# Attention: the value products of four units in one group on TensorE, with six probability buffers

## The chip, the cores and the metric

The kernel runs on one core of a Trainium2 chip. Its time is the device time of one execution in microseconds, from the first to the last instruction and the little that lies around them. Three engines matter here: TensorE (PE) multiplies matrices and writes to PSUM, VectorE (DVE) takes row maxima, ScalarE (ACT) takes exponentials and copies projections out of PSUM. GpSimd (POOL) prepares blocks of queries, SyncE (SP) issues the DMAs. The engines run their own instruction streams and wait for each other by semaphores.

## The reference, cut to what matters

Four layers, each an attention over 1444 context keys and a feed-forward part, on x of 32 batches x 100 tokens x 128. Three of the four attentions (a0, a1 and a3) have 16 heads of 8 columns and use the code that is changed; a2 is another function. In a0, for each batch:

```python
qh = proj(q, Wq, bq); kh = proj(k, Wk, bk); vh = proj(v, Wv, bv)      # 16 heads x 8
scores = jnp.einsum('bhqd,bhkd->bhqk', qh, kh) / jnp.sqrt(8)
attn = jax.nn.softmax(scores, axis=-1)                                # over 1444 keys
out = jnp.einsum('bhqk,bhkd->bhqd', attn, vh)                         # the value products
return concat @ Wo.T + bo
```

a1 masks keys by an integer mask (zeros take the place of the scores there), and a3 masks by a length per batch.

## The kernel before, in words

`attention_phase` (from L195) is called for a0, a1 and a3, one after the other, with other work between them. Each call goes through 32 batches. A batch has 24 units: two halves of eight heads, and for each half twelve tiles of 128 keys (the twelfth has 36 keys). The loop over units in `block.tensor` (from L926) writes out TensorE's order by hand. In unit u of batch b it issues:

- one maximum product, `max_mm` (L838): queries x 480 or 482 keys, into one of three PSUM banks, the ring `p_mx` (`RING = 3`). VectorE takes the row maximum from the bank (L657 in a0, L665 in a1, L671 in a3) and frees it. These products belong to the unit 16 units ahead (`LEAD`), 48 of them in a batch.
- the scores of the unit, `score_mm` (L853): two products of 400 columns into one of two PSUM slots, `p_sc`. In a1 two small products add the mask (L867). ScalarE then takes the exponential of 128 x 800 into a buffer of `probs` (L550, in a3 L548).
- in some units a small job of the batch before or after: the turned output at unit 2 (L890), `concat_turn` at 5, the output projection at 8 (L902, L904), the negated maxima at 9 and 21 (L835), in a1 `u_proj` at 13 (L827), the projection of queries at 18 (L817). They use the ring `p_mx` too, and VectorE reads them; the longest of these reads is `normalise` (L705), which VectorE does between the two maxima of unit 2.
- the second maximum product.
- in every even unit the value products, `pv_mm` (L871), of the two units before: 4 matmuls a unit, each with 32 columns of weights, side by side in the four column quarters of the array, 200 columns long in f32. In the trace each f32 matmul stands as two, so two units are 16 rows of L879. They add up in one bank, `p_pv`, over a half, and ScalarE copies it out (L536).
- in units 9, 11, 13 and 15 a projection of the next values and keys: `v01` and `v2` (L810), `k0` and `k12` (L803). They go into the two slots `p_sc` too, in turn with the scores, and ScalarE copies them out (L527 for values; L509 or L511 for keys, twice each).

What sets the order of waiting: a product into the ring waits until the third turn before it was read (`ring`, L787). A product into `p_sc` waits until the second turn before it was read (`slot`, L792). The exponential of a unit waits for its scores, and for the value products that last read its buffer:

```python
NP = 4                                                     # L230
wait_some(act, pv_done, at - NP + 1)                       # L543
```

In the text below "unit 12" is the turn of the loop with u = 12, and "a pair" is an even unit with the odd one after it.

Of the kernel before, what the change touches and what calls it, by code (L numbers as in the profile page):

```python
# [14 lines left out]
B = 32  # L15
# [9 lines left out]
UNITS = 2 * KT  # L25
# [26 lines left out]
class Memory:  # L52
# [7 lines left out]
    def sb(self, name, shape, dt=F32):  # L60
        return self.ctx.enter_context(self.nc.sbuf_tensor(f"{self.prefix}_{name}", shape, dt))
# [133 lines left out]
def attention_phase(nc, name, x, xnT, ident, w, dram, scale, gate, mask=None, lens=None):  # L195

    with ExitStack() as ctx:
# [29 lines left out]
        nm = sb("nm", [S, 2, HALF])  # L227
        nmsp = sb("nmsp", [S, 2, 32], F32R)
        nsb = sb("nsb", [D, S])
        NP = 4  # L230
        probs = sb("probs", [D, NP, HALF * S])
        osb = sb("osb", [D, 2, 2 * S])
        rs = sb("rs", [S, 2, HALF])
# [112 lines left out]
        def p_slot(*job):  # L346
            return p_sc[sc_turn[job] % 2]

        def wait_some(eng, signal, count):
            if count > 0:  # L350
                eng.wait_ge(signal, count)

        def full(eng, *job):

            if job in mx_turn:
                eng.wait_ge(mx_full, mx_turn[job] + 1)
            else:
                eng.wait_ge(sc_full, sc_turn[job] + 1)

        def taken(eng, *job):  # L360

            if job in mx_turn:
                eng.wait_ge(mx_free, mx_turn[job] + 1)
            else:
                eng.wait_ge(sc_free, sc_turn[job] + 1)
# [127 lines left out]
        def _(act):  # L493
# [44 lines left out]
            def exps(b, u):  # L538
# [3 lines left out]
                full(act, "exp", at)  # L542
                wait_some(act, pv_done, at - NP + 1)  # L543
                out_ = probs[0:rows, u % NP, :].rearrange("p (g n) -> p g n", g=2)
                in_ = p_slot("exp", at)[0:rows, :, 0:4 * S]
# [237 lines left out]
        def _(pe):  # L783
# [37 lines left out]
            def u_proj(b):  # L821
                to = ring("u", b)
                taken(pe, "v2", b)
                pe.wait_ge(gone_ready, b + 1)
                for t in range(KT):
                    r = D if t < KT - 1 else LAST
                    ins = pe.matmul(to[0:S, 0:HEADS * 9].rearrange("p (h d) -> p h d", h=HEADS),  # L827
                                    gone[0:r, b % 2, t, :], v_aug[0:r, b % 2, t, :, 0:9],
                                    start=(t == 0), stop=(t == KT - 1))
                ins.then_inc(mx_full, 1)  # L830

            def neg_turn(b, h):
                to = ring("neg", 2 * b + h)
                pe.wait_ge(negm_ready, 2 * b + h + 1)
                pe.matmul(to[96:128, 0:S], nmsp[:, h, :].bitcast(F32), ident[0:S, 0:S],  # L835
                          start=True, stop=True).then_inc(mx_full, 1)

            def max_mm(k):  # L838
                b, r = divmod(k, 2 * UNITS)
                if b >= B:  # L840
                    return
                h, r = divmod(r, 2 * KT)
                head, c = divmod(r, NCH)
                o, n = CHUNKS[c]
                if r == 0:
                    pe.wait_ge(stack_in[b % 2][h], (b // 2 + 1) * 96)
                    pe.wait_ge(qblk_ready, 2 * b + h + 1)
                to = ring("max", k)
                g = 2 * h + head // 4
                pe.matmul(to[0:S, 0:n], qblk[0:96, b % 2, HALF * h + head, :], stack[0:96, b % 2, g, o:o + n],  # L850
                          start=True, stop=True).then_inc(mx_full, 1)

            def score_mm(b, u):  # L853
                h, kt = divmod(u, KT)
                r = D if kt < KT - 1 else LAST
                if kt == 0:
                    pe.wait_ge(qneg_ready, 2 * b + h + 1)
                if u == 0 and mask is not None:
                    pe.wait_ge(pen_ready, b + 1)
                to = slot("exp", UNITS * b + u)  # L860
                for g in range(2):
                    out_ = to[0:r, g, 0:4 * S]
                    ins = pe.matmul(out_, stack[:, b % 2, 2 * h + g, kt * D:kt * D + r],  # L863
                                    qblk[:, b % 2, HALF * h + 4 * g:HALF * h + 4 * g + 4, :].rearrange("p h s -> p (h s)"),
                                    start=True, stop=mask is None)
                    if mask is not None:
                        ins = pe.matmul(out_.rearrange("p (h s) -> p h s", h=4), identb[0:r, 0:r],  # L867
                                        bc(pen[0:r, b % 2, kt, :], 1, 4), start=False, stop=True)
                ins.then_inc(sc_full, 1)

            def pv_mm(b, u):  # L871
                h, kt = divmod(u, KT)
                r = D if kt < KT - 1 else LAST
                taken(pe, "exp", UNITS * b + u)
                if kt == 0:
                    wait_some(pe, pv_out, 2 * b + h)
                for t in range(4):
                    head = HALF * h + 2 * t
                    ins = pe.matmul(p_pv[32 * t:32 * t + 32, 0:2 * S],  # L879
                                    v_aug[0:r, b % 2, kt, head:head + 2, :].rearrange("p h d -> p (h d)"),  # L880
                                    probs[0:r, u % NP, 2 * t * S:2 * (t + 1) * S],
                                    start=(kt == 0), stop=(kt == KT - 1))
                ins.then_inc(pv_done, 1)

            def out_turn(b):
                to = ring("out", b)
                pe.wait_ge(pv_out, 2 * b + 2)
                for a in range(2):
                    for h in range(2):
                        ins = pe.transpose(to[0:S, a * 256 + h * D:a * 256 + (h + 1) * D],  # L890
                                           osb[:, h, a * S:(a + 1) * S], ident[:, :])
                ins.then_inc(mx_full, 1)

            def concat_turn(b):
                to = ring("concat", b)
                pe.wait_ge(norm_ready, b + 1)
                pe.transpose(to[:, 0:S], concat[:, :], ident[0:S, 0:S]).then_inc(mx_full, 1)

            def out_proj(b):
                to = ring("wo", b)  # L900
                taken(pe, "concat", b)
                ins = pe.matmul(to[0:S, 0:D], ctsb[:, :], wo[:, :], start=True, stop=bo is None)  # L902
                if bo is not None:
                    ins = pe.matmul(to[0:S, 0:D], ones_row[:, :], bo[:, :], start=False, stop=True)  # L904
                ins.then_inc(mx_full, 1)
# [19 lines left out]
            for b in range(B):  # L925
                for u in range(UNITS):  # L926
                    g = UNITS * b + u + LEAD
                    max_mm(2 * g)
                    score_mm(b, u)
                    if b > 0:  # L930
                        if u == OUT_AT:
                            out_turn(b - 1)
                        if u == CONCAT_AT:
                            concat_turn(b - 1)
                        if u == WO_AT:
                            out_proj(b - 1)
                    if u == NEG1_AT:
                        neg_turn(b, 1)
                    if u == U_AT and mask is not None and b + 1 < B:
                        u_proj(b + 1)  # L940
                    if u == Q_AT and b + 2 < B:
                        q_proj(b + 2)
                    if u == NEG0_AT and b + 1 < B:
                        neg_turn(b + 1, 0)
                    max_mm(2 * g + 1)
                    if u % 2 == 0 and (b > 0 or u > 0):
                        for back in (2, 1):
                            at = UNITS * b + u - back
                            pv_mm(at // UNITS, at % UNITS)
                    if u == V01_AT and b + 1 < B:  # L950
                        v_proj("v01", b + 1)
                    if u == V2_AT and b + 1 < B:
                        v_proj("v2", b + 1)
                    if u == K0_AT and b + 2 < B:
                        k_proj("k0", b + 2)
                    if u == K12_AT and b + 2 < B:
                        k_proj("k12", b + 2)
            pv_mm(B - 1, UNITS - 2)
            pv_mm(B - 1, UNITS - 1)
            out_turn(B - 1)  # L960
            concat_turn(B - 1)
            out_proj(B - 1)
# [1278 lines left out]
```

## Time and profile before

| | |
|---|---|
| median of 3 runs | 6742.71 us (6737.07 to 6746.94) |
| profiled execution | 6736.52 us, span 6734.7 us |
| busy, share of the span | PE 88%, PE weight loads 60%, DVE 70%, ACT 52%, POOL 29% |
| granted TensorE clock, mean | 0.938 |
| a0, a1 and a3 at full clock | about 1283, 1707 and 1348 us |
| value products L879 | 18432 rows, 1051.8 us busy |

A busy share of PE is not PE at its peak: matmuls are pipelined, and the end of one is modelled. What counts in the rows are the starts. In a timeline a row gives its start and length in us, then engine, line, operation, what is written and read, shapes and the number of instructions merged in the row; in brackets how long the engine had been idle before it, and who ended that.

### The profile page before, as it was taken

The page shows a single profiled execution, that of the slowest core. Times are in us where ns is not written, and L with a number is a line of the kernel's source. Part 1 is how long each engine was busy: PE and PEld are TensorE (multiplying, and loading weights), DVE is VectorE, ACT ScalarE, POOL GpSimd, SP SyncE. Part 2 cuts the span into 40 slices and gives each one's busy share as a digit, 9 for nine tenths or more (in the row PEclk, how much of TensorE's full clock was granted, in tenths as well). Part 3 has the DMA queues.
Part 4 walks back from the last instruction along what each step waited for, and adds up shares of the span by engine and source line. Part 5 has one row for each costly group of instructions (what it writes and reads, how often), then busy time and mean ns, then how long its engine had stood idle before and what let it go on. Part 6 is the DMA issues. An engine that isn't in the chain of part 4 may idle for free. (4 is left out here: it accounts for less than half of the span.)

```text
span 6734.7 us, 123692 instructions
## 1 busy us (share of the span) xinstructions
PE 5947.1 (88%) x42776; PEld 4044.1 (60%) x42776; DVE 4732.6 (70%) x12652; ACT 3471.3 (52%) x5250; POOL 1972.7 (29%) x1415
## 2 busy tenths in 40 slices
PE   6999999969897999999999956768498799999996
PEld 4666666659894555555555545645388466566653
DVE  6878777867676666666666676634577777777775
ACT  3666666655553444444444433423255466666664
POOL 2222222224453222222222122334255222222220
PEclk9999999989997999999999977878699799999998
DMA  3333333220002333333333132356332333232321
GB/s 75 77 78 73 72 72 75 63 68 21 21 21 68 81 77 81 78 79 75 76 79 75 35 68 52 60 157 183 98 118 81 82 72 71 67 69 68 69 67 25
DMA packets 200964, 492.88 MB, mean 73 GB/s; under 512 B 31689, under 2 KB 135318, under 8 KB 199162
## 3 DMA queue, kind: packets, MB, share of 16 engines
q1 hardware_dynamic: 200386, 485.47, 29.5%
q8 instruction: 327, 5.36, 0.3%
q14 instruction: 251, 2.06, 0.1%
HBM read 270.18 MB, written 2.25 MB: 40 GB/s over the span
## 5 line engine op out<-in xcount | busy, mean ns | idle before, releaser
L850 PE MATMUL a_max<-a_stack,a_qblk 96*100 96x482 f32 (+1 forms) x4608 | 2003.5, 455 | 114.3 <-DVE a_mx L671 35.7
L550 ACT ACTIVATE a_probs<-a_scores 128x800 f32<-128x800 f32 (+1 forms) x1536 | 1281.3, 838 | 1019.0 <-PE a_scores L867 656.9
L863 PE MATMUL a_scores<-a_qblk,a_stack 128*128 128x400 f32 (+1 forms) x4608 | 1378.7, 372 | 8.1 <-POOL a_qblk L455 2.7
L665 DVE CUSTOM_DVE_ANT_0 a_dump<-a_max,a_mqf 100x482 f32<-100x482 f32 (+1 forms) x1536 | 978.5, 657 | 426.4 <-PE a_max L850 395.6
L850 PEld LDWEIGHTS a_max<-a_stack,a_qblk 96*100 96x100 f32 x4608 | 767.2, 167 | 745.1 <-issue 205.6
L671 DVE CUSTOM_DVE_ANT_0 a_dump<-a_max,a_penq 100x482 f32<-100x482 f32 (+1 forms) x1536 | 955.6, 657 | 280.9 <-PE a_max L850 261.7
L657 DVE TENSOR_REDUCE a_mx<-a_max 100x1 f32<-100x482 f32 (+1 forms) x1536 | 941.4, 654 | 257.6 <-PE a_max L850 239.8
L879 PE MATMUL a_pv<-a_probs,a_v_aug 128*32 128x200 f32 x18432 | 1051.8, 340 | 3.4 <-ACT a_probs L548 2.1
L863 PEld LDWEIGHTS a_scores<-a_qblk,a_stack 128*128 128x128 f32 (+1 forms) x4608 | 840.4, 186 | 185.6 <-issue 52.7
L1165 POOL TENSOR_TENSOR f_hb<-f_hb,f_wb 128x400 f32<-128x400 f32 x560 | 655.8, 1185 | 965.1 <-DVE f_hb L1413 490.2
L548 ACT ACTIVATE a_probs<-a_scores,a_kbias 128x800 f32<-128x800 f32 (+1 forms) x768 | 697.5, 926 | 413.6 <-PE a_scores L863 413.4
L431 POOL TENSOR_TENSOR a_klo<-a_kf,a_khi 128x1444 fp32r<-128x1444 f32 x96 | 316.0, 3292 | 1511.0 <-ACT a_khi L511 1067.9
L879 PEld LDWEIGHTS a_pv<-a_probs,a_v_aug 128*32 128x32 f32 x18432 | 458.5, 108 | 475.5 <-issue 309.4
L455 POOL TENSOR_TENSOR a_qblk<-a_nsb,a_blk 32x800 fp32r<-32x800 f32 x192 | 292.4, 1523 | 1519.2 <-DVE a_nsb L697 1514.7
L1419 DVE TENSOR_TENSOR f_hl<-f_hb,f_hh 128x400 fp32r<-128x400 f32 x632 | 426.7, 675 | 248.3 <-ACT f_hh L1217 245.4
L1217 ACT ACTIVATE f_hh<-f_hb 128x400 fp32r<-128x400 f32 x632 | 339.9, 538 | 437.1 <-POOL f_hb L1165 399.7
L867 PE MATMUL a_scores<-a_pen,a_identb 128*128 128x400 bf16 (+1 forms) x1536 | 528.4, 344 | 0.0
L1497 PE MATMUL f_y<-f_hh,f_wd_lo 128*128 128x400 f32 x632 | 242.0, 383 | 217.9 <-DVE f_hl L1419 149.9
L445 POOL TENSOR_TENSOR a_qblk<-a_qs,a_blk 96x400 fp32r<-96x400 f32 x384 | 319.3, 851 | 87.9 <-PE a_scores L867 56.6
L1413 DVE TENSOR_TENSOR f_hb<-f_u,f_gs 128x400 f32<-128x400 f32 x496 | 281.7, 568 | 72.0 <-ACT f_gs L1229 67.8
L867 PEld LDWEIGHTS a_scores<-a_pen,a_identb 128*128 128x128 bf16 (+1 forms) x1536 | 147.0, 96 | 297.4 <-issue 296.6
L1229 ACT ACTIVATE f_gs<-f_g 128x400 f32<-128x400 f32 x496 | 247.8, 500 | 136.1 <-PE f_u L1499 128.3
(302 smaller groups left out, 8471.7 us busy)
## 6 DMA issues: line engine op xcount, KB each, us to landing
a_stack<-a_khi SPq DMA_DIRECT2D x768, 180.5 KB, 3.4
a_ctxT<-in_ctxT_dram SPq DMA_DIRECT2D x128, 722.0 KB, 8.5
a_stack<-a_klo SPq DMA_DIRECT2D x384, 180.5 KB, 3.5
f_wb<-weights_by_token SPq DMA_DIRECT2D x24, 1600.0 KB, 10.7
f_wb<-weights_by_token SPq DMA_DIRECT2D x64, 400.0 KB, 6.3
a_ctxn<-in_ctxn_dram SPq DMA_DIRECT2D x32, 704.0 KB
a_mt_i<-in_mask1T_dram SPq DMA_DIRECT2D x32, 600.0 KB, 6.9
a_mq_i<-in_mask_dram SPq DMA_DIRECT2D x32, 564.1 KB
```

The source lines that it names most:

```text
L548: act.activation(out_, in_, ACT.Exp, bias=kbias[0:rows, b:b + 1, kt], scale=scale).then_inc(sc_free, 1)
L550: act.activation(out_, in_, ACT.Exp, scale=scale).then_inc(sc_free, 1)
L657: nc.vector.tensor_reduce(out_, src, AX.X, ALU.max).then_inc(mx_free, 1)
L665: nc.vector.tensor_tensor_reduce(dump[:, k % 2, 0:n], src, mqf[:, b % 2, o:o + n], 1.0, -3.0e38, ALU.mult, ALU.max, out_).then_inc(mx_free, 1)
L671: nc.vector.tensor_tensor_reduce(dump[:, k % 2, 0:n], src, penq[:, b % 2, o:o + n], 1.0, -3.0e38, ALU.add, ALU.max, out_).then_inc(mx_free, 1)
L850: pe.matmul(to[0:S, 0:n], qblk[0:96, b % 2, HALF * h + head, :], stack[0:96, b % 2, g, o:o + n], start=True, stop=True).then_inc(mx_full, 1)
L863: ins = pe.matmul(out_, stack[:, b % 2, 2 * h + g, kt * D:kt * D + r], qblk[:, b % 2, HALF * h + 4 * g:HALF * h + 4 * g + 4, :].rearrange( ...
L867: ins = pe.matmul(out_.rearrange("p (h s) -> p h s", h=4), identb[0:r, 0:r], bc(pen[0:r, b % 2, kt, :], 1, 4), start=False, stop=True)
L879: ins = pe.matmul(p_pv[32 * t:32 * t + 32, 0:2 * S], v_aug[0:r, b % 2, kt, head:head + 2, :].rearrange("p h d -> p (h d)"), probs[0:r, u % ...
L1165: pool.tensor_tensor(hb[:, slot(n, c), :], hb[:, slot(n, c), :], wb[:, q, row, :], ALU.mult).then_inc(hw_ready, 1)
L1217: act.activation(hh[:, half(n, c), :], hb[:, slot(n, c), :], ACT.Copy).then_inc(hh_ready, 1)
L1419: nc.vector.tensor_tensor(hl[:, half(n, c), :], hb[:, slot(n, c), :], hh[:, half(n, c), :].bitcast(F32), ALU.subtract).then_inc(hl_ready, 1)
```

## The change

The value products are done in every fourth unit (0, 4, 8, 12, 16, 20) for the four units before, and `probs` has six buffers instead of four. The exponential of a unit now waits for the value products of the unit six before it. After the last batch four units' products are done together. The number of every instruction stays the same.

```diff
-        NP = 4
+        NP = 6
         probs = sb("probs", [D, NP, HALF * S])
...
                     max_mm(2 * g + 1)
-                    if u % 2 == 0 and (b > 0 or u > 0):
-                        for back in (2, 1):
+                    if u % 4 == 0 and (b > 0 or u > 0):
+                        for back in (4, 3, 2, 1):
                             at = UNITS * b + u - back
                             pv_mm(at // UNITS, at % UNITS)
...
-            pv_mm(B - 1, UNITS - 2)
-            pv_mm(B - 1, UNITS - 1)
+            for u in range(UNITS - 4, UNITS):
+                pv_mm(B - 1, u)
```

TensorE's order in a0 from the start of unit 10 to the value products of unit 12 (L850 maximum, L863 scores, L879 value products, L810 value projection v2), before:

```order
L850 MATMUL a_max<-a_stack,a_qblk 100x482
L863 MATMUL a_scores<-a_qblk,a_stack 128x400 x2
L850 MATMUL a_max<-a_stack,a_qblk 100x482
L879 MATMUL a_pv<-a_probs,a_v_aug 32x200 x8
L850 MATMUL a_max<-a_stack,a_qblk 100x480
L863 MATMUL a_scores<-a_qblk,a_stack 36x400 x2
L850 MATMUL a_max<-a_stack,a_qblk 100x482
L810 MATMUL a_scores<-a_wv,a_ctxT 128x128 x4
L850 MATMUL a_max<-a_stack,a_qblk 100x482
L863 MATMUL a_scores<-a_qblk,a_stack 128x400 x2
L850 MATMUL a_max<-a_stack,a_qblk 100x480
L879 MATMUL a_pv<-a_probs,a_v_aug 32x200 x8
```

The same place in the changed kernel:

```order
L850 MATMUL a_max<-a_stack,a_qblk 100x482
L863 MATMUL a_scores<-a_qblk,a_stack 128x400 x2
L850 MATMUL a_max<-a_stack,a_qblk 100x482
L850 MATMUL a_max<-a_stack,a_qblk 100x480
L863 MATMUL a_scores<-a_qblk,a_stack 36x400 x2
L850 MATMUL a_max<-a_stack,a_qblk 100x482
L810 MATMUL a_scores<-a_wv,a_ctxT 128x128 x4
L850 MATMUL a_max<-a_stack,a_qblk 100x482
L863 MATMUL a_scores<-a_qblk,a_stack 128x400 x2
L850 MATMUL a_max<-a_stack,a_qblk 100x480
L879 MATMUL a_pv<-a_probs,a_v_aug 32x200 x16
```

The eight value matmuls of unit 10 are gone from there and stand with those of unit 12; the scores of unit 11 now follow those of unit 10 with two maximum products between them.

TensorE's order in a0 from the start of unit 14 to the start of unit 16 (L803 is the key projection k12), before:

```order
L850 MATMUL a_max<-a_stack,a_qblk 100x480
L863 MATMUL a_scores<-a_qblk,a_stack 128x400 x2
L850 MATMUL a_max<-a_stack,a_qblk 100x482
L879 MATMUL a_pv<-a_probs,a_v_aug 32x200 x8
L850 MATMUL a_max<-a_stack,a_qblk 100x482
L863 MATMUL a_scores<-a_qblk,a_stack 128x400 x2
L850 MATMUL a_max<-a_stack,a_qblk 100x480
L803 MATMUL a_scores<-a_ctxT,a_wk 128x482 x2
L850 MATMUL a_max<-a_stack,a_qblk 100x482
```

And in the changed kernel:

```order
L850 MATMUL a_max<-a_stack,a_qblk 100x480
L863 MATMUL a_scores<-a_qblk,a_stack 128x400 x2
L850 MATMUL a_max<-a_stack,a_qblk 100x482 x2
L863 MATMUL a_scores<-a_qblk,a_stack 128x400 x2
L850 MATMUL a_max<-a_stack,a_qblk 100x480
L803 MATMUL a_scores<-a_ctxT,a_wk 128x482 x2
L850 MATMUL a_max<-a_stack,a_qblk 100x482
```

Here too the value products between unit 14 and unit 15 are gone, and move to unit 16. On ScalarE and VectorE the order of the instructions is unchanged.

## Rows read from the trace of the kernel before

**Rows 1.** Page, part 1 and part 5: busy time, and the value products.

```profile
PE 5947.1 (88%) x42776; PEld 4044.1 (60%) x42776; DVE 4732.6 (70%) x12652; ACT 3471.3 (52%) x5250; POOL 1972.7 (29%) x1415
...
L879 PE MATMUL a_pv<-a_probs,a_v_aug 128*32 128x200 f32 x18432 | 1051.8, 340 | 3.4 <-ACT a_probs L548 2.1
```

**Rows 2.** Busy time by stretch: a0, a1, a3; granted clock (PEclk), DMA share, GB/s last.

```profile
99.20:1382.60 1283.40, 1274.77 (x10746) 823.03 (x10738) 1010.71 (x1972) 805.99 (x1073) 326.72 (x243) 1.00 0.31 70
2157.50:3864.00 1706.50, 1670.32 (x12905) 950.07 (x12903) 1146.65 (x3705) 837.55 (x1162) 422.04 (x273) 1.00 0.31 74
5301.10:6649.00 1347.90, 1291.31 (x10663) 805.47 (x10662) 1055.92 (x3497) 852.14 (x1072) 326.93 (x243) 1.00 0.29 67
```

**Rows 3.** Timeline of PE in a0, second half of unit 6 to unit 8.

```profile
428.03 0.38 PE L850 MATMUL a_max<-a_stack,a_qblk 96*100 96x480 f32 x1
428.34 0.89 PE L879 MATMUL a_pv<-a_probs,a_v_aug 128*32 128x200 f32 x16
429.16 0.47 PE L850 MATMUL a_max<-a_stack,a_qblk 96*100 96x482 f32 x1
429.46 0.53 PE L863 MATMUL a_scores<-a_qblk,a_stack 128*128 128x400 f32 x2
429.83 0.60 PE L850 MATMUL a_max<-a_stack,a_qblk 96*100 96x482 f32 x2
430.27 0.52 PE L863 MATMUL a_scores<-a_qblk,a_stack 128*128 128x400 f32 x2
```

**Rows 4.** Timeline of DVE in a0, units 1 to 7 of the same batch.

```profile
420.84 1.82 DVE L657 TENSOR_REDUCE a_mx<-a_max 100x1 f32<-100x482 f32 x3 [0.36 <-PE a_max L850]
422.57 0.20 DVE L722 RECIPROCAL a_rs<-a_max 100x8 f32<-100x8 f32 x1
...
423.18 0.23 DVE L726 TENSOR_TENSOR a_concat<-a_max,a_rs 100x64 f32<-100x64 f32 x1
423.64 3.66 DVE L657 TENSOR_REDUCE a_mx<-a_max 100x1 f32<-100x482 f32 x6 [0.24 <-DVE a_concat L726]
...
429.66 1.25 DVE L657 TENSOR_REDUCE a_mx<-a_max 100x1 f32<-100x482 f32 x2 [0.43 <-PE a_max L850]
```

**Rows 5.** Timeline of PE's weight loads in a0: start of unit 4, scores of unit 17.

```profile
424.35 0.16 PEld L850 LDWEIGHTS a_max<-a_stack,a_qblk 96*100 96x100 f32 x1 [0.32 <-DVE a_mx L657]
...
408.61 0.30 PEld L863 LDWEIGHTS a_scores<-a_qblk,a_stack 128*128 128x128 f32 x2 [0.39 <-ACT a_khi L509]
```

**Rows 6.** Timeline in a0, value projection v01 to the start of unit 12.

```profile
433.90 1.95 PE L810 MATMUL a_scores<-a_wv,a_ctxT 128*128 128x128 f32 x16
...
435.58 0.17 PEld L850 LDWEIGHTS a_max<-a_stack,a_qblk 96*100 96x100 f32 x1
...
435.89 1.09 ACT L527 ACTIVATE a_v_aug<-a_scores 128x512 f32<-128x512 f32 x2 [1.63 <-PE a_scores L810]
...
436.86 0.84 ACT L550 ACTIVATE a_probs<-a_scores 128x800 f32<-128x800 f32 x1
...
439.08 0.17 PEld L850 LDWEIGHTS a_max<-a_stack,a_qblk 96*100 96x100 f32 x1
```

**Rows 7.** Timeline in a0, unit 14 to the start of unit 16.

```profile
401.71 0.16 PEld L850 LDWEIGHTS a_max<-a_stack,a_qblk 96*100 96x100 f32 x1 [0.21 <-DVE a_mx L657]
...
402.17 0.35 PEld L863 LDWEIGHTS a_scores<-a_qblk,a_stack 128*128 128x128 f32 x2 [0.30 <-ACT a_probs L550]
402.31 0.66 ACT L509 ACTIVATE a_kf<-a_scores,a_bk 128x480 f32<-128x480 f32 x1 [0.19 <-PE a_scores L803]
...
402.87 0.65 ACT L509 ACTIVATE a_khi<-a_scores,a_bk 128x480 fp32r<-128x480 f32 x1
...
403.42 0.83 ACT L550 ACTIVATE a_probs<-a_scores 128x800 f32<-128x800 f32 x1
...
405.94 0.16 PEld L850 LDWEIGHTS a_max<-a_stack,a_qblk 96*100 96x100 f32 x1 [0.22 <-issue]
```

**Rows 8.** DVE by line inside a1 and a3: busy, mean ns, idle before.

```profile
L665 DVE CUSTOM_DVE_ANT_0 a_dump<-a_max,a_mqf 100x482 f32<-100x482 f32 x1150 | 734.3, 657 | 323.3 <-PE a_max L850 299.2 <-DVEq L727 10.1 <-DVE a_mx L665 5.3
...
L671 DVE CUSTOM_DVE_ANT_0 a_dump<-a_max,a_penq 100x482 f32<-100x482 f32 x1125 | 700.9, 657 | 197.4 <-PE a_max L850 183.4 <-DVE a_mx L671 4.9 <-issue 0.3
```

## The prediction

> **What bounds the kernel now.** I read the busy times first, then the stretches of the three attentions, then timelines of one batch, engine by engine. The page gives PE 88% of the span [rows 1]. In the three attentions PE is close to always busy (1274.77 of 1283.40 us in a0), DVE is busy for 79%, 67% and 78%, ACT for less, and the clock is granted in full throughout (1.00, the level of 2.4 GHz) [rows 2]. So the path is PE's own stream, and the question is which part of it is work and which is gaps. The timeline of PE shows that [rows 3]. A maximum product that follows another in a row takes 0.22 us (two in 430.27 - 429.83 = 0.44), and the two scores 0.37 (429.83 - 429.46). But from the maximum to the value products it is 0.31 (428.34 - 428.03), and after them the first maximum takes 0.30 until the scores follow (429.46 - 429.16), not 0.22. The group of value products itself takes 0.82 (429.16 - 428.34).
>
> DVE is close behind. Back to back its maxima start every 0.58 us (three in 1.82, the last of 0.65) [rows 4], so 48 of them are 28 us of a batch of about 40.6 (a0, between like places of two batches). It still waits 0.43 us for PE after a group of value products (429.66), 0.50 after the product began [rows 3, 4]. When it is PE that waits for DVE, the weight load comes 0.71 after the start of the maximum that frees the bank (424.35 against 423.64) [rows 4, 5].
>
> **What the change saves on PE.** A group of two units costs 0.82, plus 0.31 - 0.22 = 0.09 in front of it and 0.30 - 0.22 = 0.08 behind: 0.99. Leaving it out and doing its products in the next group adds four rounds there (two units x 2 passes of 200 columns, four quarters side by side). A pass of 128 columns takes (1.95 - 0.28)/15 = 0.112 us in the value projection [rows 6], so 200 columns take 0.175 and four rounds 0.70. Saved per pair of groups: 0.99 - 0.70 = 0.29, say 0.30. A batch has 12 groups before and 6 after: 6 x 0.30 = 1.80 us. Over 3 x 32 batches: **-173 us**. That is all the change can save, since it removes no instruction.
>
> The Trainium skill ("TensorEngine Tiling (Array Packing)", Key Properties) says that changing the tiling mode drains TensorE. The trace agrees: 0.09 and 0.08 us stand on the two sides of each group, and some 0.1 more in its 0.82.
>
> **What it costs.** The pairs without a group lose 0.99 us of PE time and the others gain 0.70. Both the maxima and the scores of a short pair then come sooner than DVE and ACT have freed their banks. The long pairs starve DVE instead. I went through one batch of a0 unit by unit with the durations above. Three waits take the saving back.
>
> (1) ACT's copies of projections. They take the same two slots as the scores, and until now the group of value products lay over them. Unit 10 starts at 435.6; v01 is copied until 435.89 + 1.09 = 436.98 [rows 6]. The scores of unit 11 need that slot. Without the group PE is ready for them at 435.6 + 0.89 + 0.22 = 436.7, but can load at 437.03 and stream at 437.19: 0.47 lost. v2 behind them needs the exponential of unit 10, done at 437.70, and starts at 437.94 instead of 437.78: 0.16 more. Its 0.81 us end at 438.75, before 439.08. The pair saves 0.34 and not 0.99; 0.65 is a wait. Units 14 and 15: k0 is copied until 402.87 + 0.65 = 403.52 [rows 7], the load follows 0.05 later (as it does for unit 14: exponential done 402.12, load 402.17; and for unit 17 behind k12 [rows 5]), so the scores of unit 15 stream at 403.73. PE would be ready at 403.14: 0.59. k12 then waits 0.17 for the exponential that ends at 403.42 + 0.83. In all 0.76. Against that the old wait of unit 17 for k12's copy (0.39 idle [rows 5]) goes, since the group of unit 16 is longer: -0.35. Sum for a0: 1.08 us a batch. In a3 the exponentials are 0.09 longer, but some of these waits exist already: 1.04. In a1 the mask products give each unit 0.37 more on PE, which covers most: 0.41. Together 2.53 x 32 = **+81 us**.
>
> (2) `normalise`. DVE does it between the two maxima of unit 2, and it ends at 423.41; the next maximum starts at 423.64 and frees the bank for unit 4 at 424.35 [rows 4, 5]. The group of unit 2 lies inside that time. Without it unit 4 still starts at 424.35, so units 2 and 3 save nothing, while unit 4 gets its 0.70: the 0.99 is all lost. It is so in all three (in a1 and a3 the step is longer still). 2.94 x 32 = **+94 us**.
>
> (3) The ring of three banks. A short pair has four maxima, 4 x 0.58 = 2.32 us for DVE, but PE needs 1.62 for it. PE can be only three banks ahead. From the maximum before a group of four units to the next it is 0.31 + 0.82 + 0.70 = 1.83, and DVE gets it 0.50 later, at 2.33. Its three banks last until 1.6: it stands idle for 0.7 per group, where it was 0.43. After that it must catch up while PE waits. Units 22 and 23 of a0 as the example, from the start of unit 22: DVE takes up the second maximum of unit 21 at 0.33 (its first came 0.50 after unit 21 began, and the copy of the negated maxima is between), then those of unit 22 at 0.91 and 1.49. PE is ready for unit 23 at 0.30 + 0.37 + 0.22 = 0.89, but its bank is free at 0.33 + 0.71 = 1.04. For unit 0 it would be ready at 1.04 + 0.89 = 1.93, and the bank is free at 1.49 + 0.71 = 2.20. Without waits of DVE the pair would be 0.89 + 0.81 = 1.70; so 0.50 is lost. By the walk the pairs (18,19), (22,23) and (6,7) of a0 take 0.37, 0.50 and 0.24 longer than PE alone would; 0.16 more at starts of units 0 and 8; 0.17 comes back at unit 21, where PE waits for DVE now. Sum 1.10. In a3, with maxima of 0.657 and the same step of 0.58 [rows 8], more of it exists already (the wait of unit 21 there is 0.42): 0.71. In a1 a unit without a group takes PE 1.17 to 1.25, as long as two maxima take DVE, and DVE waits 299.2 us for PE in the stretch [rows 8]: -0.06. Together 1.75 x 32 = **+56 us**.
>
> Bounds. None of these waits is seen in the trace, only the durations that make them. (1) could be near 0 if ACT got its copies done sooner than its order lets it, and up to 1.6 a batch in each (154 us) if the later exponentials push the next ones. (2) is between 0.7 and 1.1 a batch: 67 to 106 us. (3) is between -0.17 x 64 = -11 us, where only the old wait goes, and 0.7 - 0.43 idle more at each group plus the catching up, some 1.8 a batch in a0 and a3 and 0.5 in a1: 131 us. I take the values of the walk, since they lie between, and each rests on neighbouring rows.
>
> Six buffers cost nothing: the exponential of unit 4k+2 is the first that needs the products of unit 4k-4, and these stand in the group of unit 4k, in front of its scores on PE anyway. The last value products of the kernel's attentions get two units longer, 0.35 x 3 = 1 us. The turned outputs and the copy of `p_pv` (units 1 and 13 on ACT) need the groups of units 0 and 12, which stay. SP's and POOL's queues have nothing moved in them.
>
> **The sum.** -173 + 81 + 94 + 56 = **+58 us**. In the profiled execution (6736.5 us, 6 below the median) that gives 6795; from the median of 6743 it gives 6800. By phases: a0 1.34 us a batch slower (+43), a3 0.92 (+29), a1 0.47 faster (-15).
>
> **Rivals.**
> A. PE alone sets the time and all of the saving comes through: 6743 - 173 = 6570. For it speaks PE's 99% in a0 [rows 2]; against it that the overlap of DVE and ACT is from the groups themselves, as the rows of (1) and (2) show. By the rule of the page above on drains this is what would happen, 576 drains fewer. Chance 0.04.
> B. Only `normalise` and the ring count, and ACT's copies do not hold PE up: 58 - 81 = -23, so 6720, faster by 0.3%. For it: DVE is the busier engine. Against it: unit 14 waits for ACT already [rows 7]. Chance 0.10.
> C. The terms cancel: (1) and (3) 30% smaller each, 58 - 41 = 17 us, or a little less: within 13 us of 6743. Chance 0.10.
> D. Slower by far: the value products come too soon for the exponential of the unit before. In rows of a0 it is done 1.41 us after its scores begin (0.57 until it starts, 0.84 long), and between two short units PE asks for it after 0.37 + 0.22 + 0.22 + 0.37 + 0.31 = 1.49. The slack is 0.08, gone as soon as ACT is behind by one copy. Where it fails by 0.3 at each of the 576 groups: +173, so 6970. From a slack below 0.08 on it decides. The walk has it covered by the other waits of PE. Chance 0.06.
>
> **Numbers.** The forecast has 0.70: 6800, itself between 6765 and 6840. Slower by over 0.2% (13 us, about what a measurement of this kernel tells from none) is the forecast and D: 0.76. Same is C, 0.10; faster is A and B, 0.14. The range reaches from between B and C to past the forecast's upper bounds: 6735 to 6860.
>
> **What would show it.** PE's first maximum after a group of four starts 1.52 us after the group, and there are half as many such groups. New rows of PE waiting for ACT's value copy (L527) before the scores of unit 11, and for the key copy before those of unit 15. The pair of units 2 and 3 as long as before, 3.1 us in a0. DVE idle about 0.7 after each group. A batch of a0 42.0 us instead of 40.6, one of a1 not longer. It is wrong if a0 gets shorter, if the pair (10,11) saves its full 0.99, or if the granted clock in the three attentions falls below 1.00.

## The result, and the profile after

The changed kernel takes 6836.91 us (median of 4 runs, 6829.58 to 6840.78) against 6744.82 (4 runs, 6737.07 to 6757.22): a ratio of 1.0133 with a 95% interval of 1.0115 to 1.0152, or +92 us. It is slower, as forecast, inside the range, and by 34 us more than the +58 of the sum. Of all the runs reported below one, the fourth of `six_buffers_groups_of_two`, took 10337.88 us at a mean clock of 0.831, and the ratios leave it out.

The busy times of the changed kernel, the page's first part and its rows of the value products and of the maximum products, answer to [rows 1]:

```profile
PE 5938.6 (87%) x42776; PEld 4099.2 (60%) x42776; DVE 4766.6 (70%) x12652; ACT 3474.1 (51%) x5250; POOL 1972.1 (29%) x1415
...
L850 PE MATMUL a_max<-a_stack,a_qblk 96*100 96x482 f32 (+1 forms) x4608 | 1971.2, 455 | 185.3 <-DVE a_mx L671 53.8
...
L879 PE MATMUL a_pv<-a_probs,a_v_aug 128*32 128x200 f32 x18432 | 955.4, 344 | 0.0
```

The maximum products in the kernel before:

```profile
L850 PE MATMUL a_max<-a_stack,a_qblk 96*100 96x482 f32 (+1 forms) x4608 | 2003.5, 455 | 114.3 <-DVE a_mx L671 35.7
```

The value products' own busy time fell by 96 us (from 1051.8), with the same count, and PE's idle time in front of the maximum products grew by 71 (114.3 to 185.3). Yet the span grew by 98. The busy time by stretch, columns as in [rows 2], for a0, a1 and a3 of the changed kernel; each stretch begins and ends within some 7 us of the same point of the program as before:

```profile
99.00:1426.80 1327.80, 1278.83 (x10749) 831.03 (x10747) 1012.24 (x1972) 806.02 (x1072) 326.33 (x243) 1.00 0.30 68
2204.60:3887.20 1682.60, 1627.47 (x12815) 974.34 (x12813) 1146.20 (x3682) 835.89 (x1157) 422.57 (x273) 0.99 0.31 74
5354.90:6744.70 1389.80, 1310.20 (x10595) 822.17 (x10594) 1051.60 (x3469) 849.51 (x1066) 326.54 (x243) 0.98 0.28 65
```

In a0 PE is now idle for 49 us of its stretch (1327.80 - 1278.83) where it was 9. And the granted clock is no longer full in a1 and a3.

From the first to the last maximum product a0 takes 1332.4 us (before 1290.2), a1 1707.7 (1721.3), a3 1408.6 (1360.0): +42, -14 and +49. The remaining +21 lie between a1 and a3, in code that is the same. That stretch takes 1422 to 1449 us over the ten profiles of this study (1428 before, 1449 here), in no order with the changes, so I read it as spread. The medians differ by +92, so 15 more than the +77 of the three attentions; where these 15 lie the one profiled execution of each kernel does not show.

The lengths of pairs of units tell where the time goes. These are means over batches 3 to 28, from the starts of the maximum products (L850) in the two traces, in us:

| pair | a0 before, after | a1 | a3 |
|---|---|---|---|
| 0, 1 (group) | 2.74, 3.50 | 3.47, 4.16 | 2.76, 3.50 |
| 2, 3 | 3.12, 3.13 | 4.64, 4.64 | 3.55, 3.55 |
| 4, 5 (group) | 3.01, 3.69 | 4.03, 5.00 | 4.07, 5.40 |
| 6, 7 | 2.69, 2.02 | 3.42, 2.44 | 2.68, 2.11 |
| 8, 9 (group) | 5.55, 6.28 | 5.91, 6.45 | 5.56, 6.01 |
| 10, 11 | 3.50, 3.07 | 4.70, 3.71 | 3.50, 3.15 |
| 12, 13 (group) | 3.26, 3.93 | 7.31, 8.00 | 3.37, 3.93 |
| 14, 15 | 4.22, 3.92 | 4.95, 3.96 | 4.51, 3.82 |
| 16, 17 (group) | 3.34, 3.66 | 3.71, 4.39 | 3.15, 3.65 |
| 18, 19 | 3.29, 2.75 | 4.02, 3.15 | 3.31, 2.83 |
| 20, 21 (group) | 3.23, 3.97 | 4.26, 5.02 | 3.66, 4.23 |
| 22, 23 | 2.68, 2.12 | 3.88, 2.89 | 2.68, 2.16 |
| batch | 40.6, 42.0 | 54.3, 53.8 | 42.8, 44.3 |

A group of four itself is as worked out. The timeline of PE in the changed kernel, a0, unit 8, answers to [rows 3]:

```profile
441.39 0.46 PE L850 MATMUL a_max<-a_stack,a_qblk 96*100 96x482 f32 x1
441.78 1.57 PE L879 MATMUL a_pv<-a_probs,a_v_aug 128*32 128x200 f32 x32
443.27 0.46 PE L850 MATMUL a_max<-a_stack,a_qblk 96*100 96x482 f32 x1
```

It takes 443.27 - 441.78 = 1.49 us for 32 rows (1.52 was forecast), where two groups of 16 took 1.64. DVE pays for it. Its timeline at the same place, answering to the last of [rows 4], and again after the group of unit 12:

```profile
443.77 0.66 DVE L657 TENSOR_REDUCE a_mx<-a_max 100x1 f32<-100x482 f32 x1 [0.72 <-PE a_max L850]
...
452.49 1.25 DVE L657 TENSOR_REDUCE a_mx<-a_max 100x1 f32<-100x482 f32 x2 [1.37 <-PE a_max L850]
```

After the group of unit 12 in the kernel before:

```profile
441.55 1.24 DVE L657 TENSOR_REDUCE a_mx<-a_max 100x1 f32<-100x482 f32 x2 [0.69 <-PE a_max L850]
```

DVE is idle for 0.72 us instead of 0.43 after the group of unit 8, and for 1.37 instead of 0.69 after that of unit 12, to which it comes with fewer maxima left to take.

The new waits for ACT, in the timeline of the changed kernel at the places of [rows 6] and [rows 7]:

```profile
446.61 1.08 ACT L527 ACTIVATE a_v_aug<-a_scores 128x512 f32<-128x512 f32 x2 [1.63 <-PE a_scores L810]
...
447.74 0.14 PEld L863 LDWEIGHTS a_scores<-a_qblk,a_stack 128*36 128x36 f32 x2 [0.57 <-ACT a_v_aug L527]
...
448.47 0.97 PEld L810 LDWEIGHTS a_scores<-a_wv,a_ctxT 128*128 128x128 f32 x8 [0.35 <-ACT a_probs L550]
...
454.45 0.65 ACT L509 ACTIVATE a_khi<-a_scores,a_bk 128x480 fp32r<-128x480 f32 x1
...
455.15 0.30 PEld L863 LDWEIGHTS a_scores<-a_qblk,a_stack 128*128 128x128 f32 x2 [0.70 <-ACT a_khi L509]
```

The load of the scores of unit 11 comes 0.05 after ACT's last copy of v01 (446.61 + 1.08 = 447.69), and that of unit 15 0.05 after the copy of k0 (455.10). Neither wait exists in [rows 6, 7].

What I had not foreseen is in unit 4 of a3. First a batch without it, then the batch after, PE's timeline of the changed kernel:

```profile
5878.53 0.47 PE L850 MATMUL a_max<-a_stack,a_qblk 96*100 96x482 f32 x1 [0.63 <-DVE a_mx L671]
5878.93 1.56 PE L879 MATMUL a_pv<-a_probs,a_v_aug 128*32 128x200 f32 x32
5880.42 0.46 PE L850 MATMUL a_max<-a_stack,a_qblk 96*100 96x480 f32 x1
...
5921.00 0.46 PE L850 MATMUL a_max<-a_stack,a_qblk 96*100 96x482 f32 x1 [0.58 <-DVE a_mx L671]
5921.30 0.53 PE L863 MATMUL a_scores<-a_qblk,a_stack 128*128 128x400 f32 x2
5922.46 0.72 PE L850 MATMUL a_max<-a_stack,a_qblk 96*100 96x482 f32 x1 [0.63 <-DVE a_mx L671]
5923.11 2.89 PE L879 MATMUL a_pv<-a_probs,a_v_aug 128*32 128x200 f32 x32
5925.93 0.72 PE L850 MATMUL a_max<-a_stack,a_qblk 96*100 96x480 f32 x1
```

The same group takes 1.49 us in the one and 2.82 in the other, and a maximum product 0.72 instead of 0.47. The stretches around the two units, with the granted clock in the third column from the end:

```profile
5921.00:5929.00 8.00, 7.37 (x46) 4.58 (x46) 4.95 (x15) 1.91 (x3) 0.00 (x0) 0.57 0.01 2
...
5877.00:5882.00 5.00, 4.03 (x42) 2.50 (x43) 4.11 (x15) 1.66 (x3) 0.00 (x0) 1.00 0.00 1
```

The clock was at its lower level, 1.2 GHz (0.50 granted), from 5921.90 to 5928.70. In the 3.40 us before that PE was busy for 2.63, and it had stood idle for 0.58 us waiting for VectorE in front of 5921.00. The batch before has the same waits (0.57 and 0.63 us) and kept the full clock, so what decides in which batch it falls is not shown. The Trainium skill ("TensorE: Matmul & The Clock Gate", HAM oscillation — how this bites in real kernels) says that waits of PE between bursts of work can bring the lower clock back, so that the next work starts slowly. This trace agrees, though the waits of the page's example are for DMA and longer, and here each one is for VectorE and some 0.6 us. Unit 4 of a3 is slow (4.7 to 4.9 us instead of 3.35) in 13 of the 30 batches from batch 1 on, and takes 4.17 in one more; in the kernel before there is none. In a1 it is slow (4.4 to 4.9 us instead of 3.29) in 8. In a0, past its start, the clock does not fall.

### The profile page after: what moved, and what is told of

Its sections match the earlier page's. It is cut to its first block and busy times, and to the rows that moved or that the text cites. A ratio compares the mean times of both kernels' runs of the same rounds, so it can differ in the third digit from the quotient of the medians.

```text
span 6832.4 us, 123688 instructions
## 1 busy us (share of the span) xinstructions
PE 5938.6 (87%) x42776; PEld 4099.2 (60%) x42776; DVE 4766.6 (70%) x12652; ACT 3474.1 (51%) x5250; POOL 1972.1 (29%) x1415
## 5 line engine op out<-in xcount | busy, mean ns | idle before, releaser
L850 PE MATMUL a_max<-a_stack,a_qblk 96*100 96x482 f32 (+1 forms) x4608 | 1971.2, 455 | 185.3 <-DVE a_mx L671 53.8
L863 PE MATMUL a_scores<-a_qblk,a_stack 128*128 128x400 f32 (+1 forms) x4608 | 1381.7, 372 | 27.1 <-ACT a_khi L509 8.4
L850 PEld LDWEIGHTS a_max<-a_stack,a_qblk 96*100 96x100 f32 x4608 | 768.1, 168 | 811.1 <-issue 240.0
L665 DVE CUSTOM_DVE_ANT_0 a_dump<-a_max,a_mqf 100x482 f32<-100x482 f32 (+1 forms) x1536 | 962.4, 656 | 406.6 <-PE a_max L850 382.3
L671 DVE CUSTOM_DVE_ANT_0 a_dump<-a_max,a_penq 100x482 f32<-100x482 f32 (+1 forms) x1536 | 939.9, 656 | 326.8 <-PE a_max L850 304.5
L657 DVE TENSOR_REDUCE a_mx<-a_max 100x1 f32<-100x482 f32 (+1 forms) x1536 | 924.9, 653 | 298.7 <-PE a_max L850 283.7
L863 PEld LDWEIGHTS a_scores<-a_qblk,a_stack 128*128 128x128 f32 (+1 forms) x4608 | 842.4, 186 | 227.7 <-issue 43.9
L879 PE MATMUL a_pv<-a_probs,a_v_aug 128*32 128x200 f32 x18432 | 955.4, 344 | 0.0
L879 PEld LDWEIGHTS a_pv<-a_probs,a_v_aug 128*32 128x32 f32 x18432 | 528.0, 111 | 362.2 <-issue 153.2
L445 POOL TENSOR_TENSOR a_qblk<-a_qs,a_blk 96x400 fp32r<-96x400 f32 x384 | 320.7, 854 | 42.8 <-PE a_scores L867 26.9
L803 PE MATMUL a_scores<-a_ctxT,a_wk 128*128 128x482 f32 (+1 forms) x576 | 279.4, 595 | 46.8 <-DVE a_ones_row L615 28.2
```

Of the source, the lines that this page charges most:

```text
L657: nc.vector.tensor_reduce(out_, src, AX.X, ALU.max).then_inc(mx_free, 1)
L665: nc.vector.tensor_tensor_reduce(dump[:, k % 2, 0:n], src, mqf[:, b % 2, o:o + n], 1.0, -3.0e38, ALU.mult, ALU.max, out_).then_inc(mx_free, 1)
L671: nc.vector.tensor_tensor_reduce(dump[:, k % 2, 0:n], src, penq[:, b % 2, o:o + n], 1.0, -3.0e38, ALU.add, ALU.max, out_).then_inc(mx_free, 1)
L879: ins = pe.matmul(p_pv[32 * t:32 * t + 32, 0:2 * S], v_aug[0:r, b % 2, kt, head:head + 2, :].rearrange("p h d -> p (h d)"), probs[0:r, u % ...
```

## The experiments

All kernels below keep the six buffers. Where groups are set freely, the loop reads

```diff
-                    if u % 4 == 0 and (b > 0 or u > 0):
-                        for back in (4, 3, 2, 1):
+                    if u in GROUP_AT and (b > 0 or u > 0):
+                        before = [v for v in GROUP_AT if v < u]
+                        n = u - before[-1] if before else UNITS - GROUP_AT[-1]
+                        for back in range(n, 0, -1):
```

so that each group does the units since the last one. Ratios are to the kernel before, on the same chip.

**The buffers alone.** `GROUP_AT = tuple(range(0, 24, 2))`.

> Six probability buffers, but the value products of two units in every even unit as before. Theory (the grouping alone makes the change slower; the wait of an exponential for its buffer is never the last one, with four buffers or six): the time of the kernel before, 6745 us, within 0.2%. Rival (the buffers do something by themselves: ACT runs further ahead, or the larger tile moves others): 6745 minus or plus more than 13 us, and then the same part of the +92 is theirs.

Measured 6737.79 us, ratio 0.9994 (0.9979 to 1.0009), and the pairs of a0 and a1 within 0.01 us of before. So the grouping makes the change slower, and not the buffers. One pair of a3 does differ: (14,15) takes 4.36 us with six buffers and 4.51 with four, where every other batch has some 0.28 more. That is worth 5 us in a3, less than the runs tell apart, and its cause stays open.

**One group put back.** `GROUP_AT = (0, 2, 4, 8, 12, 16, 20)`.

> The changed kernel with one group put back: groups stand in units 0, 2, 4, 8, 12, 16 and 20, so units 2 and 3 of each batch have the group of two units inside the time of normalise again, and the group of unit 4 does two units in place of four. Theory (normalise covers a group of unit 2; without it PE also stands so long that the granted clock drops in unit 4): unit 2 and 3 stay at 3.13 us in a0, unit 4 gets 0.70 shorter, 96 x 0.70 = 67 us, and the dips of the clock inside a1 and a3 go (31 us in the trace of the changed kernel): 6837 - 98 = 6740. Rival (PE's own work is what counts, each group put back costs 0.29): 6837 + 96 x 0.29 = 6865. If the dips are not from PE's standing in units 2 to 4, they stay: 6770.

Measured 6731.62 us, ratio 0.9983 (0.9969 to 0.9996). More work on PE (96 groups more) and less time: by 105 us from the medians, by some 101 from the two ratios, which each compare with the kernel before at the same time. Units 2 and 3 take 3.13 us as before, units 4 and 5 3.01 in place of 3.69 in a0, and past the start of a1 and a3 no dip of the clock is left in them. PE's timeline in unit 4 of a3:

```profile
5618.96 0.47 PE L851 MATMUL a_max<-a_stack,a_qblk 96*100 96x482 f32 x1 [0.62 <-DVE a_mx L672]
5619.36 0.89 PE L880 MATMUL a_pv<-a_probs,a_v_aug 128*32 128x200 f32 x16
5620.17 0.47 PE L851 MATMUL a_max<-a_stack,a_qblk 96*100 96x480 f32 x1
```

The wait of 0.62 for DVE is the same as in the changed kernel (0.63), so the group of unit 2 cost nothing: it was done while `normalise` ran.

**Two other groups put back.** `GROUP_AT = (0, 4, 8, 10, 12, 14, 16, 20)`.

> The changed kernel with the groups of units 10 and 14 put back, which lie over ACT's copies of v01 and k0: groups in units 0, 4, 8, 10, 12, 14, 16 and 20. Theory (without them the scores of units 11 and 15 wait for these copies, so in a0 and a3 the two groups were nearly free, in a1 they were not): by the pair lengths of the two traces a0 changes by -0.25 us a batch, a3 by -0.03, a1 by +0.60, together +10 us: 6847, and no wait of PE for L527 before the scores of unit 11. Rival (each group put back costs PE its 0.29): 6837 + 192 x 0.29 = 6893.

Measured 6836.19 us, ratio 1.0156 (1.0139 to 1.0173). Against the changed kernel that is nothing by the medians (6836.91) and 15 us more by the ratios; the maximum products of the two traces give +15 too (-7 in a0, +21 in a1, +1 in a3). That is near the +10 of the expectation and far from the +56 of its rival. The four pairs from 10 to 17 are back at the values of before (3.50, 3.25, 4.22, 3.33 in a0), a batch of a0 is 0.26 us shorter, one of a1 0.80 longer. Of that 0.61 is in the four pairs: in a1 the two groups had been merged at a gain. The rest is in units 4 and 5, where the clock fell oftener in this run. The weight loads of a0 by line (busy us, mean ns, idle before, and who ended it), first here, then in the changed kernel, in the same stretch of 300 to 1275 us:

```profile
L864 PEld LDWEIGHTS a_scores<-a_qblk,a_stack 128*128 128x128 f32 (+1 forms) x1124 | 203.5, 183 | 42.6 <-ACT a_khi L510 9.0 <-ACT a_probs L551 6.8 <-issue 5.5
```

```profile
L863 PEld LDWEIGHTS a_scores<-a_qblk,a_stack 128*128 128x128 f32 x1117 | 200.6, 183 | 61.0 <-ACT a_khi L509 16.3 <-ACT a_v_aug L527 13.2 <-ACT a_probs L550 6.8
```

The 13.2 us behind L527, 0.57 for each of some 23 batches, are gone with the group put back. Behind the key copy, 16.3 us fall to 9.0, about what the kernel before has there for unit 17 (9.3).

**More work for PE in its waits.**

```diff
-                for g in range(2):
+                again = (3 if lens is not None else 2 if mask is not None else 1) if u == 3 else 2 if u == 4 and lens is not None else 1
+                for g in (0, 1) * again:
                     out_ = to[0:r, g, 0:4 * S]
```

> The changed kernel, with the two score products of unit 3 done three times over in a3 and twice in a1, those of unit 4 twice in a3 (the result is overwritten with the same), all of it inside the time in which PE waits for normalise and the row masks. Theory (the slow groups of unit 4, 4.8 instead of 3.35 us in 14 of 31 batches of a3 and 4.5 to 4.8 instead of 3.29 in 8 of a1, are PE at the lower clock level after a stretch with little work): the dips of the clock inside a1 and a3 go, though PE does more: 6837 - 31 = 6806. Rival (the slow groups have another cause, such as a wait inside the group): no dip goes, and the time is 6837 or longer by what the extra products (0.37 us each pair) cost.

Measured 6791.17 us, ratio 1.0073 (1.0048 to 1.0097), less than the changed kernel by 46 us from the medians and by 40 from the ratios. The stretch of a3 past its start has the full clock again, where the changed kernel has 0.98; first this run, then the changed kernel:

```profile
5375.00:6700.00 1325.00, 1273.41 (x10438) 820.94 (x10438) 1019.94 (x3367) 822.25 (x1031) 316.02 (x235) 1.00 0.29 66
```

```profile
5375.00:6723.00 1348.00, 1272.75 (x10248) 799.11 (x10247) 1035.80 (x3417) 820.24 (x1030) 320.21 (x240) 0.98 0.29 66
```

Units 4 and 5 take 4.75 us in a3 (mean 5.40 in the changed kernel, its median 4.76) and 4.70 in a1 (5.00). By the maximum products a1 gets 12 us shorter and a3 19: the 31 of the expectation. The other 10 to 15 us lie between the attentions or within the spread of the runs, which I cannot tell apart.

**A faster VectorE.** The maxima are taken over 240 or 241 of the 480 or 482 columns; the other half is left out. Once with groups of two and once with groups of four.

```diff
                 o, n = CHUNKS[c]
                 full(dve, "max", k)
+                n = n // 2
```

> VectorE takes each maximum over the first half of the columns only (240 or 241), so it has about half the work for the ring; groups of two units as in the kernel before. It is the partner of the next run. Both theories: about as long as before or some us shorter, since PE is the bound there: 6700 to 6745.

> The changed kernel with each maximum taken over the first half of the columns only. Theory (the lost part of the saving in units 6-7, 18-19 and 22-23 is PE waiting for DVE in the ring of three banks): against the run with groups of two and half maxima, the pairs (18,19), (22,23) of a0 get 0.9 to 1.0 us shorter, where they got 0.54 and 0.56 shorter with full maxima; the pair (10,11), which waits for ACT, still gets only 0.43 shorter. In all a0 changes by 0.0 to +0.3 us a batch in place of +1.39, and the whole kernel by -20 to +25 us in place of +92. Rival (the pairs wait for something other than DVE, or the ring is deep enough): the pairs save the same 0.54 and 0.56, and the difference of the two runs stays at +65 or more.

Measured 6601.0 us (ratio 0.9783, 0.9764 to 0.9803) with groups of two. That missed its expectation: I had taken the kernel before as bound by PE alone, but PE's waits for DVE in it are worth some 140 us, half of it in a3 (42.8 to 40.6 us a batch). With groups of four 6597.73 (ratio 0.9778, 0.9759 to 0.9797): the grouping now costs -3 us and not +92. The pair (22,23) of a0 goes from 2.60 to 1.61, (6,7) from 2.67 to 1.69: the full 0.99. (18,19) goes from 3.29 to 2.50, a little less than said. (10,11) goes from 3.50 to 3.07, the same 0.43 as with full maxima, since it waits for ACT. A batch of a0 gets 0.14 us longer (+1.39 with full maxima). The faster DVE does not keep the clock up everywhere: in a3 it no longer falls, but in a1 it still does in unit 4 of some batches. The start of unit 23 in a0, PE's timeline with half maxima and then in the changed kernel:

```profile
449.42 0.60 PE L851 MATMUL a_max<-a_stack,a_qblk 96*100 96x482 f32 x2
449.86 0.53 PE L864 MATMUL a_scores<-a_qblk,a_stack 128*36 128x400 f32 x2
450.23 0.61 PE L851 MATMUL a_max<-a_stack,a_qblk 96*100 96x482 f32 x2
```

```profile
468.27 0.78 PE L850 MATMUL a_max<-a_stack,a_qblk 96*100 96x482 f32 x2
468.89 0.52 PE L863 MATMUL a_scores<-a_qblk,a_stack 128*36 128x400 f32 x2
469.25 0.94 PE L850 MATMUL a_max<-a_stack,a_qblk 96*100 96x482 f32 x2
```

Two maximum products and the scores behind them begin 0.44 us apart in the first and 0.62 in the second; the next two take 0.61 and 0.94. PE waits for a bank there, as its weight loads in the changed kernel show:

```profile
468.60 0.16 PEld L850 LDWEIGHTS a_max<-a_stack,a_qblk 96*100 96x100 f32 x1 [0.34 <-DVE a_mx L657]
...
469.73 0.16 PEld L850 LDWEIGHTS a_max<-a_stack,a_qblk 96*100 96x100 f32 x1 [0.40 <-DVE a_mx L657]
```

**A version that beats both.** In a1 PE has the most work per unit, and DVE and ACT are hardly late but in units 2 and 3: the other five short pairs save 0.88 to 0.99 us each. Groups of four there, with the group of unit 2 kept, and groups of two in a0 and a3:

```diff
+        GROUP_AT = tuple(range(0, 24, 2)) if mask is None else (0, 2, 4, 8, 12, 16, 20)
```

> Groups in units 0, 2, 4, 8, 12, 16 and 20 in a1 (the attention whose PE work per unit is longest), groups of two in a0 and a3. Theory (there PE is behind DVE and ACT, so that five of the six merged groups give their saving, as the pair lengths of a1 in the trace with the group of unit 2 kept show: 52.8 in place of 54.3 us a batch): -50 us, 6741 - 50 = 6691, and 6680 to 6700. Rival (the gain of a1 is a matter of the run): 6741.

Measured 6689.63 us (6 runs, 6676.82 to 6700.49), ratio 0.9925 (0.991 to 0.994). By the maximum products the gain is 1721.3 - 1673.9 = 47 us in a1, and a0 and a3 are as in the kernel with six buffers and groups of two.

**One merged group in a3 too.** `GROUP_AT` of a3 without unit 6.

> As groups_of_four_in_a1_alone, and in a3 the group of unit 6 is merged into that of unit 8 too (pairs (6,7) and (8,9): -0.59 and +0.46 us in the two traces). Theory: 4 us less than that run, about 6687; the difference is below what a measurement tells. Rival (a merged group in a3 costs): 6695 or more.

Measured 6691.24 us, ratio 0.992 (0.9906 to 0.9934). Pairs (6,7) and (8,9) of a3 do change by -0.59 and +0.46 us, but the 4 us that this makes are not seen beside the run before it. Inconclusive as a time.

## Why the prediction was right, and by how much it was off

The path and the three waits were as said, but for ACT's in a1. That the sum came as near as it did is in part luck: of its terms one was too large, one too small and one was missing. The terms by the pairs of the table above, in us a batch; a short pair without any wait saves 0.99 and a long one costs 0.68. The measured sum, +78, is the +77 of the three attentions within rounding.

| term | predicted a0, a1, a3 | measured | predicted, measured over 32 batches |
|---|---|---|---|
| saving on PE | -1.80 each | -1.86 each | -173, -179 |
| (1) ACT's copies | 1.08, 0.41, 1.04 | 0.88, 0.00, 0.77 | +81, +53 |
| (2) `normalise` | 2.94 in all | 0.99 each | +94, +95 |
| (3) the ring | 1.10, -0.06, 0.71 | 1.39, 0.06, 1.02 | +56, +79 |
| the clock | none | 0, 0.31, 0.64 | 0, +30 |
| sum | | | +58, +78 |

- **The saving on PE.** Predicted 0.29 to 0.30 for each merged pair of groups. Where nothing waits, the lengths give 0.99 - 0.68 = 0.31 (a1, pairs 14,15 and 16,17), and with a faster DVE the short pairs of a0 give 0.99. Right.
- **ACT's copies.** Predicted 0.65 and 0.76 us lost in pairs (10,11) and (14,15) of a0, less 0.35 won back at unit 17, which makes 1.06 and not the 1.08 of the sum. Measured: the pairs save 0.43 and 0.31 of 0.99, so 0.56 and 0.68, and pair (16,17) costs 0.32 instead of 0.68, so 0.36 back: 0.88. The mechanism is right in a0 and a3, and the run with the two groups put back shows it. It was wrong in a1, where 0.41 was predicted: both pairs there save their full 0.99 (4.70 to 3.71, 4.95 to 3.96), so PE lost nothing to the copies. That the pair (10,11) saves its full 0.99 was one of the prediction's own signs of being wrong.
- **`normalise`.** Predicted that units 2 and 3 save nothing in any attention. They changed by less than 0.01 us in all three. Right, and shown by the run with that group kept.
- **The ring.** Predicted 1.10 us a batch in a0. By the pairs 18 to 23, 0, 1 and 6 to 9 it is 1.39. Right in its place, a fifth too small; the 0.17 that was to come back at unit 21 did not, since pair (20,21) grew by 0.74. The half maxima show that it is DVE in a0. In a1 and a3 the term is what the pairs leave over when the others are taken off.
- **Sum by attention.** a0: +43 us predicted, +42 measured. a1: -15 predicted, -14 measured. a3: +29 predicted, +49 measured. The match of a1 is luck: ACT's 0.41, which did not come, stands against 0.31 of the clock, which was not in the sum. In a0 ACT's term was 0.20 too large and the ring's 0.29 too small.
- **The clock: missing.** The sum takes it that "the clock is granted in full throughout" holds in the changed kernel too; a fall stands only among the signs of being wrong, and that sign came. In a3 the mean of units 4 and 5 is 0.64 us over their median, in a1 0.31: 20 and 10 us in all. That is the gap of a3. The group inside the wait of units 2 and 3 was also what kept PE's clock up: with it put back the falls are gone, and with more scores in units 3 and 4 in its place they are gone too. Units 2 and 3 last 3.54 us in a3 and 4.64 in a1 with or without their group; in a0, where they last 3.13, the clock did not fall.
- **The rest** of the +92, some 15 us, is in no attention and is not explained; the runs of either kernel spread over 11 to 20 us.
- **The rivals.** A (all of the saving, 6570) was wrong by the ACT and DVE waits. B (ACT does not count) fell to the rows behind L527 in a0 and a3, though for a1 alone it was right. C (the terms cancel) is out by the time. D (value products too early for the exponential) did not come: the groups of four run without a break inside, 1.49 us.

## What to carry to other kernels

Work that an in-order engine does while it would wait anyway is free, and moving it out of the wait makes it cost its length elsewhere (here 0.68 us for a group of two units that had cost nothing). So before grouping small jobs to save the cost of switching, look at each place from which one is taken, and ask what the engine would wait for there: a slot, a ring, another engine's longest step. Decide it place by place, as 47 us came from one attention of three, and with the same groups the other two got longer; and count the granted clock as one of the things that such filler work buys.

## What the runs showed of the hardware that I had not expected

Doing the same scores two or three times over, inside waits, made the kernel faster (6837 to 6791 us). 31 us of that are in a1 and a3, where the granted clock then stayed at its higher level. At the lower one a group of value products took 2.82 us in place of 1.49.
